# Softmax and spreading of attention weights: one tile at a time, or a pair at a time

## The reference

```python
xn = layernorm(x)
q, k, v = (xn @ W + b).reshape(b, s, 4, 256)            # 4 heads; W: 256 x 1024
qr, qi, kr, ki = q*cos, q*sin, k*cos, k*sin             # per head and feature
scores = (qr @ kr.T + qi @ ki.T) / 16                   # between the 4 HEADS of one token
attn = softmax(scores, axis=-1)                         # 4 x 4 per token
s = (attn @ v), heads and tokens swapped, @ Wo + bo
gates = sinkhorn(router(xn)); top 2 of 8 experts        # each: relu(x@wg) * (x@wp) @ wo
x + s * silu(xn + gated sum of the two experts)
```

## Time and profile before

| | us |
|---|---|
| three runs | 1585.95, 1589.72, 1590.04 (median 1589.72) |
| the profiled execution | 1588.45 |
| its span | 1586.7 |
| PE busy | 1528.8 |
| DVE busy | 1017.2 |
| POOL busy | 795.3 |
| ACT busy | 731.9 |

### The profile page before, as it was taken

The page is one execution under the profiler, slowest core; times in us unless marked ns, Lnnn a source line. Parts: engine busy times, 40 slices in busy tenths (PEclk is TensorE's granted clock), DMA queues, the critical chain, the costliest instruction groups (busy, mean ns, idle before and its releaser), DMA issues.

```text
span 1586.7 us, 31308 instructions
## 1 busy us (share of the span) xinstructions
PE 1528.8 (96%) x10868; PEld 1141.1 (72%) x10868; DVE 1017.2 (64%) x2015; ACT 731.9 (46%) x1205; POOL 795.3 (50%) x945
## 2 busy tenths in 40 slices
PE   5999799989999999999999999999999999999997
PEld 2546666668888888888888888776666776666773
DVE  7567989954444444444444444678888888888777
ACT  5766334413333333333333333556456565555552
POOL 4648589823434443444344433262584664753456
PEclk9999799989999999999999999999999999999999
DMA  9988842265233241323111321346555566445464
GB/s 326 394 326 324 308 175 83 73 225 182 71 121 118 71 135 58 116 74 135 57 54 58 110 108 44 103 153 203 174 170 179 200 194 220 163 157 168 153 206 147
DMA packets 173298, 251.14 MB, mean 158 GB/s; under 512 B 15336, under 2 KB 122656, under 8 KB 173024
## 3 DMA queue, kind: packets, MB, share of 16 engines
q1 hardware_dynamic: 158528, 211.48, 39.0%
q0 software_dynamic: 12960, 35.41, 6.7%
q10 hardware_dynamic: 1664, 2.26, 0.4%
HBM read 149.58 MB, written 99.50 MB: 157 GB/s over the span
## 4 chain that ended last, share of the span: by engine, by line
PE 90%; DVE 5%; DMA 1%; issue 1%; ACT 1%; SPq 1%; ACTq 0%; DVEq 0%
PE ps L1151 23%; PE ps L1086 22%; PE ps L1097 13%; PE ps L1170 12%; PE ps L1033 7%; PE ps L1160 4%; PE ps L1054 2%; PE ps L1133 2%; PE ps L1002 2%; PE ps L930 1%; PE ps L986 1%; PE ps L920 1%; DVE UN L1236 1%; DMA WR<-w_d 1%; ACT WM L823 0%
## 5 line engine op out<-in xcount | busy, mean ns | idle before, releaser
L1151 PE MATMUL ps<-WR,FR 128*128 x1620 | 404.8, 399 | 2.7 <-DMA WR<-w_d 2.7
L1151 PEld LDWEIGHTS ps<-WR,FR 128*128 128x128 f32 x1620 | 295.6, 189 | 58.0 <-issue 3.0
L1663 DVE TENSOR_TENSOR AUX<-AUX,ps 128x512 f32<-128x512 f32 x135 | 92.9, 688 | 338.4 <-ACT AUX L862 338.4
L655 POOL DMA_INDIRECT y_d<-AUX x135 | 133.6, 990 | 348.7 <-DVE AUX L1652 348.4
L823 ACT ACTIVATE WM<-ps,bcs,trig 128x512 f32<-128x512 f32 x256 | 254.4, 1018 | 90.7 <-PE ps L1086 82.9
L1599 DVE TENSOR_SCALAR WM<-ps,vec,trig 128x512 f32<-128x512 f32 x256 | 245.2, 994 | 63.1 <-ACT WM L823 62.6
L1097 PE MATMUL ps<-WM,XTJ 128*128 128x512 f32 x512 | 237.1, 600 | 0.0
L862 ACT ACTIVATE AUX<-ps 128x512 f32<-128x512 f32 x135 | 81.0, 600 | 315.1 <-PE ps L1151 289.8
L1086 PE MATMUL ps<-XH,WH 128*128 128x512 f32 x512 | 206.5, 403 | 4.9 <-issue 4.0
L1170 PE MATMUL ps<-WR,ABR 128*128 x540 | 207.1, 418 | 0.0
L1086 PE MATMUL ps<-XL,WH 128*128 128x512 f32 x512 | 201.3, 393 | 0.6 <-issue 0.6
(11 more groups left out here) (239 smaller groups left out, 2255.0 us busy)
## 6 DMA issues: line engine op xcount, KB each, us to landing
US<-u_d SPq DMA_DIRECT2D x63, 512.0 KB, 4.7
u_d<-UN SPq DMA_DIRECT2D x120, 256.0 KB, 2.0
WR<-w_d SPq DMA_DIRECT2D x96, 256.0 KB
AUX<-y_d SPq DMA_DIRECT2D x32, 512.0 KB, 5.8
WM<-in_L_attn_x_dram SPq DMA_DIRECT2D x16, 512.0 KB, 9.6
xn_d<-WM SPq DMA_DIRECT2D x32, 256.0 KB, 7.4
w_d<-USR SPq DMA_DIRECT2D x16, 512.0 KB, 4.6
AUX<-xn_d SPq DMA_DIRECT2D x16, 512.0 KB, 6.1
```

The source lines that it names most:

```text
L655: e.indirect_dma_start(y_d, bass.IndirectOffsetOnAxis(toks[:, n:n + 1], 0), YS[n % 4], None).then_inc(s_y[n % 4], 16)
L1151: mm = e.matmul(b[:, :], x, WR[:, bass.ds(off[m] + (2048 * z + 1024 * a + 512 * k), 512)], start=(k == 0 and x is xh and z == 0), stop=(k ...
L1663: e.tensor_tensor(HS[:, m % 2, :], GR[:, :], mP[m % 2][:, :], ALU.mult).then_inc(s_h, 1)
```

## The change

Scores: tiles n and n + 1 (n even) go into one bank, the second into columns 256 to 511; the four tiles of a round fill banks 4 and 5, and a score tile waits only for the softmaxes of the round before. `soft_a`, `soft_b` and `spread` work on two tiles in one instruction each, with twice the elements, and ACT's exp too. `TM` is the scratch of `spread`; some small tensors move into `AC`. In steps 16 to 23 the pair 0, 1 is spread at c = 16; the pair 2, 3 at c = 20, after `mixed` of tile 1, since `AT` is written for both tiles and `spread(n + 2)` waits for mix(n + 1). In a round's softmax the order on DVE is soft_a of pair 0, soft_a of pair 2, soft_b of pair 0, soft_b of pair 2, with the marks after the two soft_a and soft_b(0). ACT does both exps and then `silu(host)`. In the last round PE does four score tiles and then four mixes.

```diff
--- before.py
+++ after.py
         i8 = sb("i8", [128, 2, E], I32)
-        SS = sb("SS", [128, 2, 16])
-        SE = sb("SE", [128, 2, 16])
+        SS, SE = (AC[:, 0, 64 * i:64 * i + 64].rearrange("p (i x) -> p i x", x=16) for i in range(2))
         SA = sb("SA", [128, 4, 16])
-        sx = sb("sx", [128, 3, 4])
+        sx = AC[:, 1, 0:24].rearrange("p (k x) -> p k x", x=8)
...
@@ -838,12 +837,12 @@
                             silu(q)
                         if q + 1 < q1 and c in (17, 20):
                             xt(q + 1, c // 20)
-                    for i in range(4):
-                        n = 4 * q + i
-                        e.wait_ge(s_sub, n + 1)
-                        e.activation(SE[:, n % 2, :], SS[:, n % 2, :], ACT.Exp, scale=1.0 / 16).then_inc(s_exp, 1)
-                        if i == 1 and q in host:
-                            silu(host[q])
+                    for n in (4 * q, 4 * q + 2):
+                        e.wait_ge(s_sub, n + 2)
+                        e.activation(SE[:, n % 4:n % 4 + 2, :], SS[:, n % 4:n % 4 + 2, :], ACT.Exp,
+                                     scale=1.0 / 16).then_inc(s_exp, 2)
+                    if q in host:
+                        silu(host[q])
             e.wait_ge(s_trig, 1)
             segment(0, QE)
 
@@ -1022,15 +1021,16 @@
                 return ps[bank(n)]
 
             def scores(n):
-                if n >= 2:
-                    e.wait_ge(s_sm1, n - 1)
+                if n >= 4:
+                    e.wait_ge(s_sm1, n - n % 4)
+                to = 256 * (n % 2)
                 for c in range(4):
                     for x in range(2):
                         for h in range(2):
                             for a in range(2):
                                 row = 64 * a
                                 col = 128 * (4 * (n % 4) + c) + row
-                                mm = e.matmul(pS[n % 2][row:row + 64, 64 * c:64 * c + 64].rearrange("p (g t) -> p g t", g=H),
+                                mm = e.matmul(pS[n % 4 // 2][row:row + 64, to + 64 * c:to + 64 * c + 64].rearrange("p (g t) -> p g t", g=H),
                                               QT[:, x, h, col:col + 64],
                                               QT[:, 2 + x, h, :].rearrange("p (g t) -> p g t", g=H)[:, :, col // 4:col // 4 + 16],
                                               start=(x == h == 0), stop=(x == h == 1))
@@ -1111,12 +1111,10 @@
                     e.wait_ge(s_cd, 16 * q + 16)
                     for i in range(4):
                         scores(4 * q + i)
-                        if q == NQ - 1 and i >= 2:
-                            mix(4 * q + i - 2)
                         place(lists.get((q, 24 + i), ()))
                 if q1 == NQ:
-                    mix(4 * NQ - 2)
-                    mix(4 * NQ - 1)
+                    for i in range(4):
+                        mix(4 * NQ - 4 + i)
 
             e.wait_ge(s_wsp, 4)
             e.wait_ge(s_mc, 18)
@@ -1480,45 +1478,46 @@
                 if 1 <= k <= 4:
                     split((0, 2, 1, 3)[k - 1])
 
-            def g4(a, n):
-                return a[:, n % 2, :].rearrange("p (c g) -> p c g", g=H)
-
-            diag = mask16[:, None, :].broadcast_to([128, 4 * H, 16])
+            def pair(a, n):
+                return a[:, n % 4:n % 4 + 2, :].rearrange("p i (c g) -> p (i c) g", g=H)
 
             def soft_a(n):
-                e.wait_ge(s_s, n + 1)
-                e.tensor_tensor(TM[:, 0:256].rearrange("p (x t) -> p x t", t=16),
-                                pS[n % 2][:, 0:256].rearrange("p (x t) -> p x t", t=16), diag,
-                                ALU.mult).then_inc(s_sm1, 1)
-                e.wait_ge(s_sm1, n + 1)
-                ch(e.tensor_reduce(SS[:, n % 2, :], TM[:, 0:256].rearrange("p (x t) -> p x t", t=16), AX.X, ALU.add))
-                ch(e.tensor_reduce(sx[:, 0, :], g4(SS, n), AX.X, ALU.max))
-                e.tensor_tensor(g4(SS, n), g4(SS, n), sx[:, 0, :, None].broadcast_to([128, 4, 4]),
-                                ALU.subtract).then_inc(s_sub, 1)
+
+                e.wait_ge(s_s, n + 2)
+                e.tensor_tensor(TM[:, :].rearrange("p (x t) -> p x t", t=16),
+                                pS[n % 4 // 2][:, :].rearrange("p (x t) -> p x t", t=16),
+                                mask16[:, None, :].broadcast_to([128, 32, 16]), ALU.mult).then_inc(s_sm1, 2)
+                e.wait_ge(s_sm1, n + 2)
+                ch(e.tensor_reduce(SS[:, n % 4:n % 4 + 2, :].rearrange("p i x -> p (i x)"),
+                                   TM[:, :].rearrange("p (x t) -> p x t", t=16), AX.X, ALU.add))
+                ch(e.tensor_reduce(sx[:, 0, :], pair(SS, n), AX.X, ALU.max))
+                e.tensor_tensor(pair(SS, n), pair(SS, n), sx[:, 0, :, None].broadcast_to([128, 8, 4]),
+                                ALU.subtract).then_inc(s_sub, 2)
 
             def soft_b(n):
-                e.wait_ge(s_exp, n + 1)
-                ch(e.tensor_reduce(sx[:, 1, :], g4(SE, n), AX.X, ALU.add))
+
+                e.wait_ge(s_exp, n + 2)
+                ch(e.tensor_reduce(sx[:, 1, :], pair(SE, n), AX.X, ALU.add))
                 ch(e.reciprocal(sx[:, 2, :], sx[:, 1, :]))
-                e.tensor_tensor(SA[:, n % 4, :].rearrange("p (c g) -> p c g", g=H), g4(SE, n),
-                                sx[:, 2, :, None].broadcast_to([128, 4, 4]), ALU.mult).then_inc(s_sa2, 1)
+                e.tensor_tensor(pair(SA, n), pair(SE, n),
+                                sx[:, 2, :, None].broadcast_to([128, 8, 4]), ALU.mult).then_inc(s_sa2, 2)
 
             def spread(n):
-                e.wait_ge(s_sa2, n + 1)
-                ch(e.tensor_tensor(AC[:, 0, :].rearrange("p (c t g) -> p c t g", c=4, g=H),
-                                   SA[:, n % 4, :].rearrange("p (c g) -> p c g", g=H)[:, :, None, :]
-                                   .broadcast_to([128, 4, 8, H]),
-                                   mask8[:, None, :, None].broadcast_to([128, 4, 8, H]), ALU.mult))
-                ch(e.transpose(AC[:, 1, :], AC[:, 0, :]))
+
+                e.wait_ge(s_sa2, n + 2)
+                ch(e.tensor_tensor(TM[:, 0:256].rearrange("p (c t g) -> p c t g", c=8, g=H),
+                                   pair(SA, n)[:, :, None, :].broadcast_to([128, 8, 8, H]),
+                                   mask8[:, None, :, None].broadcast_to([128, 8, 8, H]), ALU.mult))
+                ch(e.transpose(TM[:, 256:512], TM[:, 0:256]))
                 ch(e.tensor_reduce(AH[:, :].rearrange("p (c h) -> p c h", h=H),
-                                   AC[:, 1, :].rearrange("p (c t h) -> p c h t", c=4, h=H), AX.X, ALU.add))
-                if n >= 2:
-                    e.wait_ge(s_mx, n - 1)
-                e.tensor_tensor(AT[:, n % 2, :].rearrange("p (c r h) -> p c r h", c=4, h=H),
+                                   TM[:, 256:512].rearrange("p (c t h) -> p c h t", c=8, h=H), AX.X, ALU.add))
+                if n:
+                    e.wait_ge(s_mx, n)
+                e.tensor_tensor(AT[:, :, :].rearrange("p i (c r h) -> p (i c) r h", c=4, h=H),
                                 AH[:, :].rearrange("p (c h) -> p c h", h=H)[:, :, None, :]
-                                .broadcast_to([128, 4, 8, H]),
-                                maskr[:, None, :, None].broadcast_to([128, 4, 8, H]),
-                                ALU.mult).then_inc(s_atc, 1)
+                                .broadcast_to([128, 8, 8, H]),
+                                maskr[:, None, :, None].broadcast_to([128, 8, 8, H]),
+                                ALU.mult).then_inc(s_atc, 2)
 
             def biased(n):
                 if n == 0:
@@ -1552,7 +1551,8 @@
 
             def marks(gs):
 
-                e.wait_ge(s_disp, 1)
+                if gs:
+                    e.wait_ge(s_disp, 1)
                 for g in gs:
                         if g >= 4:
                             e.wait_ge(s_od, 4 * g - 12)
@@ -1603,11 +1603,18 @@
                             side[24 * q + c]()
                         if q > 0:
                             n = 4 * q - 4
-                            if c in (16, 18, 20, 22):
-                                spread(n + (c - 16) // 2)
-                                biased(n + (c - 16) // 2)
+                            if c == 16:
+                                spread(n)
+                                biased(n)
+                            elif c == 18:
+                                biased(n + 1)
+                            elif c == 22:
+                                biased(n + 3)
                             if c in (18, 20, 22, 23):
                                 mixed(n + (18, 20, 22, 23).index(c))
+                            if c == 20:
+                                spread(n + 2)
+                                biased(n + 2)
                         if (q, c) in firsts:
                             marks(firsts[q, c])
```

(27 more changed lines are left out.)

## The result

The changed kernel is slower: 1600.5 us median (1593.6 to 1605.2, six runs) against 1590.4 (1586.0 to 1592.2, six); the ratio is 1.0062, 95% interval 1.0042 to 1.0081. I had forecast 1586 and at most 1594. The profiled execution is the fastest of its six, 1593.61 us (span 1591.9), against 1588.45.

A forecast was written before the change was run, and what follows sets the result against it. PE, busy 96% of the span, was taken as the bound, so other engines' edits count only through its waits. Terms: -7.2 + 2.5 + 0.8 + 0.9 = -3.0, from 1588.45 to 1585.4; stated as 1586, range 1579 to 1594.

The forecast's parts named there:

- Part 1: Rounds 0 to 3: scores no longer wait for the softmax of their own round; -7.2 us, 6.3 of it in round 0.
- what they save moves all behind them: Argument against a 15% rival (early gain not real, 1590): softmaxes precede the ranks on DVE, so the ranks move earlier too.
- Part 3: Rounds 5, 7, 9, 11: silu(host) after both exps delays ACT's eviction of the next round's product 0; +0.8 us, bounds 0 and +3.
- Part 2: Rounds 4 to 15: spread of pair 2, 3 now stands behind mixed(n+1), delaying mix(2); +2.5 us, bounds 0 and +12.
- the 4.3 against 4.59: DVE's undisturbed chain from mix(1) to mix(2), 4.3 us, against PE's 4.59 between those mixes: it just fits.
- Rival A: Slower: DVE's new order stalls mix(2) in every round, at L1054 of tile 2; 1598, at half size 1594; chance 14%.
- Part 4: The tail: last round's four scores, then four mixes, partly at the lower clock level; +0.9 us, bounds -2.3 and +2.
- the missing wait at L1033: Sign of being right: score matmuls no longer wait for the mask multiply of L1490.
- the expert start at 347.2: Sign on L1151, the first expert product: right if it starts near 340 after a 7 us DMA wait, wrong after 343.
- The wait before product 9: Sign of being right: PE's wait in round 1 (L1086) grows to 5 or 6 us and ends near 182.
- The sign for part 3: Sign of being wrong: a wait at product 5 above 1 us in rounds 6, 8, 10, 12.
- The limit of 8 us at L1054: Sign of being wrong: PE's waits at the mixes (L1054) above 8 us in sum would refute part 2 and show rival A.

The follow-up runs named there:

- r1: The changed kernel run again with nothing altered: ratio 1.0061 to the kernel before.
- r9: Changed kernel with POOL's four XTJ additions for rounds 2 and 3 issued singly between groups of marks: ratio 1.0029.
- r16: Changed kernel with silu(host) at c = 23 and split POOL additions, but round 15 and the end as in the kernel before: ratio 0.9995.
- r6: Kernel before, single tiles everywhere, with only silu(host) moved behind the fourth exp of rounds 5, 7, 9, 11: ratio 1.0021.
- r5: Changed kernel with silu(host) moved behind the last V eviction (c = 23) of rounds 5, 7, 9, 11: ratio 1.0019.
- r13: Kernel before with only the spreading of rounds 0 to 14 done in pairs: ratio 1.0030.
- r17: Changed kernel with silu(host) at c = 23, split POOL additions, and tiles 56 to 59, spread in round 15, spread singly: ratio 0.9985.
- r3: Changed kernel with rounds 0 to 3 in the order of before; pairs in rounds 4 to 15 and the changed end: ratio 1.0075.
- r4: Changed kernel with round 15 alone as before, one tile at a time, first two mixes between the scores: ratio 1.0068.
- r2: Changed kernel with pairs in rounds 0 to 3 alone; rounds 4 to 15 and the end in the order of before: ratio 1.0025.
- r7: Changed kernel with the spreading of rounds 0 to 14 back to one tile at a time in its old places: ratio 1.0013.

## Why the prediction was wrong, by its steps

In short: most of what the first rounds gained was lost again before the experts, where small DVE operations now met POOL's long ones, and the late `silu(host)` held back loads. With POOL's row split and the silu moved (r10, r18) the changed kernel is at 0.9982 and 0.9998.

**Part 1 failed where it said "Everything gained before round 3 passes through" and gave 6.3 us to round 0.** DVE was free at 170.24, forecast 170.3. Then it came to the ranks of the routing earlier, beside POOL's splitting of the expert weights: 10.1 us from 174.25 to 184.35, 6.1 before. The two operations of 8 elements that took 1.11 instead of 0.17 ended within 0.03 us of an operation of POOL; L1414 below is one. DVE's eviction behind the ranks and PE's stall moved by 3.0 us, not 6.3. DVE, POOL and PE of the changed kernel, for the earlier trace rows:

```profile
170.24 4.20 DVE L1599 TENSOR_SCALAR WM<-ps,vec,trig 128x512 f32<-128x512 f32 x4
174.25 0.70 DVE L1406 COPY AUX<-ps 128x512 f32<-128x512 f32 x1
174.99 1.40 DVE L1407 TENSOR_TENSOR_SCAN AUX<-AUX 128x512 f32<-128x512 f32 x1
...
176.42 1.60 DVE L1408 TENSOR_TENSOR AUX<-AUX 128x512 f32<-128x512 f32 x1
...
178.57 1.27 POOL L621 TENSOR_TENSOR ABR<-AUX,ABR 128x512 fp32r<-128x512 f32 x1
178.76 1.11 DVE L1414 TENSOR_SCALAR i<-i 128x8 int32<-128x8 int32 x1
...
185.63 0.76 PE L1086 MATMUL ps<-XH,WH 128*128 128x512 f32 x1 [8.37 <-issue]
```

That DVE's own order is kept, "what they save moves all behind them", holds; that each operation keeps its length at another time does not. What was left went in round 2 (r1, r9). That round 3 gives nothing was right: the 4.43 of the earlier trace rows became a wait for the first tokens and the load of `WR`. Without a hit the stage takes 180.2 to 181.8 (seven of eight profiles; r16 184.9, unexplained) against 181.3 to 183.0 for the single softmax with single spreads: about 1 us gained, not 7.2.

**Part 3 failed at its first step.** It priced `silu(host)` by ACT's next eviction alone: "0.1 to 0.5 per such round". That sum was right: PE's wait there is 0.2. But I did not ask which queue stands behind the silu. SyncE's does. The loads of y_d behind it came 3.1 us later in round 6, and behind them the bias of the fourth mix, on which DVE waited 0.4 to 0.5 us in the first profile and 0.5 to 2.0 in r1. r6 puts the step at 3.3 us alone, r5 at 6.8 within the changed kernel (1.0062 to 1.0019).

**Part 2** (+2.5) had about the size of what the first profile shows (3.2) and the wrong place. Mix(2) waits 0.2, as the 4.3 against 4.59 said. But the spread of twice the width also stands ahead of the first mix, and there PE waits 0.2 to 0.6 in seven rounds, 3.2 in all (the row of L1054 for L1527 above; none of it in the earlier trace rows). Alone it measured 4.8 us (r13), with an interval of 2.4 to 7.2. Rival A had the sign and the size of the outcome (1594 to 1598) for a mechanism that isn't there.

**Part 4** (+0.9) is +2.2 in the first pair of profiles and nearly nothing over all: the ends of before's kind are 59.7, 61.5, 61.1 and 62.1 (mean 61.1), those of the changed kind 59.9 to 62.5 (nine, mean 61.2). With the old end and the pair spread they are 63.2, 63.1 and 63.9, with the new one and the single spread 58.8, 59.2, 58.5 and 61.1. These means mix two clock levels. With the new end the last two mixes ran at 0.66 to 0.68 us in eight profiles and at 1.10 or more in five. At the higher level the pair spread in round 15 gives 59.9 to 60.6 (five) and the single one 58.5 to 59.2 (three); at the lower one 61.9 to 62.5 (four) and 61.1 (r17). So that spread costs 1.1 to 1.5 and the level about 2; what the new order alone is worth stays open. The wait that answers to the earlier trace rows:

```profile
1579.97 1.11 PE L1054 MATMUL ps<-US,AT 128*32 128x256 f32 x8 [4.83 <-DVE AT L1516]
...
1588.93 0.43 DVE L1545 TENSOR_TENSOR AB<-AUX,AB 128x256 f32<-128x256 f32 x1
```

Of my signs, the missing wait at L1033 was right and proved nothing; the expert start at 347.2 was the one that told. The wait before product 9 was 8.4 us and ended at 185.6, not 5 or 6 and 182. The sign for part 3, a wait at product 5 above 1 us, stayed silent (0.2) though part 3 failed: it looked at the same engine as the sum. The limit of 8 us at L1054 was badly set, since 5.9 of its 13 us are the end's.

**The stop in round 7, and what stays open.** In r1, r3 and r4, PE stops for 2.24 to 2.79 us within round 7's first product, at its fifth matmul, which waits for no semaphore, and then runs at the lower clock. The last line is of the DMA queues from 1148.2 to 1149.4 (packets, MB, share of 16 engines):

```profile
1148.12 0.39 PE L1100 MATMUL ps<-XH,WH 128*128 128x512 f32 x1
...
1150.75 0.50 PE L1100 MATMUL ps<-XL,WH 128*128 128x512 f32 x1 [2.24 <-issue]
...
1152.07 0.63 PE L1100 MATMUL ps<-XH,WH 128*128 128x512 f32 x1
...
q8 instruction: 1, 0.02, 5.0%
```

These three kernels take 531.1 to 531.9 in rounds 4 to 15, the changed kernel's first profile and r9, without the stop, 525.9 and 526.9. It is 0.3 to 0.7 us in nine others, before among them. No engine and no semaphore is named as what it waits for, but the DMA trace has it: one packet of 16 KB on the queue `q8 instruction`, which starts and lands 0.97 and 1.93 us after the round's first product in r1. The fifth matmul starts at 3.44. In all twenty profiles the order holds: where that packet had landed 0.6 us before the round or earlier (five), the fifth matmul starts at 1.03 to 1.05; r2, where it landed at -0.27, has 1.11; and in the fourteen others it starts 1.1 to 1.5 us after the landing, which is -0.03 to 0.54 in eleven of them and 1.93 to 2.69 in r1, r3 and r4. So PE most likely waits there for its own instructions to be loaded. No run moved the packet to prove it, and why it came late in these three isn't shown; the 16 DMA engines were busy in full when it came in r1.

Round 7 alone is 3.4 of the 7.2 us between the changed kernel's two profiles, and 3.4 is also about the difference between what the late silu costs within the changed kernel (6.8) and alone (3.3; r6's profile is without the stop, as are r7's and r9's). All three with the long stop have pairs and the late silu, but r9 has both too. Whether the stop is why the parts don't add isn't shown, since each kernel has one profile or two.

## What to carry to other kernels

Before an operation is moved later in its engine's order, follow its semaphore into every queue: what counts is what stands behind the waiting instruction there, not who needs the result. Time saved early on one engine shifts all its small operations against its neighbour's, so price each at the new time by what the neighbour then runs; a row of long operations there is better broken up. Where an engine stops for nothing that the waits name, look at the instruction queue in the DMA trace. Run the change's parts alone: here two of them at 3 to 5 us each were worth 7 when taken out of the whole.

## What the hardware showed

A VectorE operation on 32 elements, 0.2 us elsewhere, took 5.1 us beside four GpSimd additions in a row, in four profiles; with GpSimd's row broken by other operations it took 1.8. The same kernel, profiled twice, differed by 5.2 us over rounds 4 to 15 and by 3.2 on the way to the experts. The end's mixes ran at 1.10 us or 0.66 each, the two clock levels, after the same 4.8 us wait. A matmul that waits for no semaphore started 1.1 to 1.5 us after a packet of the instruction queue had landed, in fourteen of twenty profiles, and held TensorE up for 2.2 to 2.8 us in three of them.
